# Twelve places instead of ten for the second stage's exponentials, in a gated cross-attention and self-attention kernel

## The reference

```python
x = x + tanh(g_xattn[0]) * xattn(layernorm(x), ctx_768, Wq, Wk, Wv, Wo, bo)
x = x + tanh(g_ffn[0]) * ffn(layernorm(x), Wq, bq, Wk, bk, Wv, bv, Wp, bp, ...)
# in ffn
q_norm = q / norm(q)
q_scaled = (q_norm + query_embedding) * softplus(temperature)
h = softmax(q_scaled @ k.T / sqrt(32)) @ v
gates = softmax(h @ Wr.T + br); top 3 of 15 routed heads, one shared head, two shared weights
out = (h * masked_gates.sum()) @ Wp.T + bp
```

## Time and profile before

| | us |
|---|---|
| median of 3 runs | 4596.27 (4593.71 to 4602.74) |
| the profiled execution | 4595.59 |
| its span, first to last instruction | 4593.8 |
| TensorE at work | 4350.3 (95%) |
| GpSimd | 3338.4 (73%) |
| VectorE | 2881.1 (63%) |
| ScalarE | 2528.2 (55%) |
| granted TensorE clock, mean | 0.985 |

### The profile page before, as it was taken

How to read it: one execution, slowest core, us unless ns; L and a number is a source line. 1 busy time by engine, 2 the same in 40 slices (tenths; PEclk the granted TensorE clock), 3 DMA queues, 4 the chain that set the end, 5 groups by cost and what they waited for, 6 DMA issues and landing times.

```text
span 4593.8 us, 67810 instructions
## 1 busy us (share of the span) xinstructions
PE 4350.3 (95%) x21568; PEld 2348.5 (51%) x21568; DVE 2881.1 (63%) x3955; ACT 2528.2 (55%) x4641; POOL 3338.4 (73%) x2667
## 2 busy tenths in 40 slices
PE   4899999999999999999999999999999999999997
PEld 3455555555555555554445444544454454544443
DVE  4455656464646464676777767676777667677661
ACT  2353535454535454546666666567557666565664
POOL 1566666767666667558888878778788879677897
PEclk7899999999999999999999999999999999999999
DMA  7476766666656666653435345354443454362532
GB/s 230 129 194 173 205 173 197 178 194 182 182 168 184 174 177 175 169 147 104 136 106 173 90 136 154 83 155 117 124 143 103 124 152 106 112 181 70 146 109 83
DMA packets 516175, 682.26 MB, mean 149 GB/s; under 512 B 42736, under 2 KB 371952, under 8 KB 506608
## 3 DMA queue, kind: packets, MB, share of 16 engines
q1 hardware_dynamic: 515824, 677.92, 52.7%
HBM read 323.57 MB, written 150.99 MB: 103 GB/s over the span
## 4 chain that ended last, share of the span: by engine, by line
PE 80%; issue 8%; ACT 4%; DVE 4%; POOL 2%; DMA 2%; SPq 0%; ACTq 0%; POOLq 0%; DVEq 0%
PE aux L957 28%; PE aux L1049 19%; PE aux L1063 18%; PE aux L1031 7%; PE aux L1075 4%; DVE nm L1404 2%; ACT probs L1247 2%; PE aux L1001 1%; POOL added_f L936 1%; PE aux L1083 1%; PE aux L977 1%; POOL added L936 1%; ACT more L1247 1%; DMA xs<-in_x 1%; DMA v_kept<-v_out 0%
## 5 line engine op out<-in xcount | busy, mean ns | idle before, releaser
L936 POOL TENSOR_TENSOR added<-added,probs 128x512 f32<-128x512 f32 x1433 | 1792.0, 1289 | 773.7 <-PE aux L1063 620.7
L1404 DVE TENSOR_REDUCE nm<-aux 128x2 f32<-128x1024 f32 x1536 | 1810.9, 1220 | 581.9 <-PE aux L1031 581.4
L1247 ACT ACTIVATE probs<-aux 128x512 f32<-128x512 f32 x2151 | 1172.3, 603 | 876.1 <-PE aux L1049 740.0
L1049 PE MATMUL aux<-stack 128*128 128x512 f32 x4096 | 1323.0, 427 | 76.5 <-ACT probs L1247 36.5
L1049 PEld LDWEIGHTS aux<-stack 128*128 128x128 f32 x4096 | 711.4, 189 | 740.7 <-issue 284.0
L1063 PE MATMUL aux<-probs,v 128*32 128x512 f32 (+1 forms) x4302 | 934.5, 610 | 4.3 <-ACT probs L1247 2.3
L936 POOL TENSOR_TENSOR added_f<-added_f,probs 128x512 f32<-128x512 f32 x537 | 672.3, 1287 | 119.6 <-PE aux L1063 73.8
L957 PE MATMUL aux<-xT_hi,wqk 128*128 128x512 f32 x1536 | 560.4, 404 | 1.0 <-ACT more L1247 0.6
L1031 PE MATMUL aux<-ck_hi,cq_hi 32*128 32x512 f32 (+1 forms) x3072 | 453.9, 483 | 53.3 <-DVE nm L1404 35.8
L1031 PEld LDWEIGHTS aux<-ck_hi,cq_hi 32*128 32x128 f32 (+1 forms) x3072 | 181.0, 185 | 512.4 <-issue 511.0
L957 PE MATMUL aux<-wvo,parts 128*128 128x512 f32 x1536 | 400.2, 403 | 10.6 <-issue 10.2
(11 more groups left out here) (132 smaller groups left out, 4387.4 us busy)
## 6 DMA issues: line engine op xcount, KB each, us to landing
wqk<-w_split SPq DMA_DIRECT2D x256, 256.0 KB, 3.8
wvo<-w_split SPq DMA_DIRECT2D x64, 1024.0 KB, 7.2
parts<-h_kept SPq DMA_DIRECT2D x128, 512.0 KB, 3.9
stack<-cq_hi SPq DMA_DIRECT2D x128, 256.0 KB, 5.2
stack<-ck_hi SPq DMA_DIRECT2D x128, 256.0 KB, 5.5
v_kept<-v_out SPq DMA_DIRECT2D x128, 256.0 KB, 2.3
v<-v_kept SPq DMA_DIRECT2D x64, 512.0 KB, 4.4
h_kept<-h_hi SPq DMA_DIRECT2D x128, 256.0 KB, 2.8
```

The lines of the kernel that those rows point to most:

```text
L936: pool.tensor_tensor(onto, onto, exp_buffer(T, e), ALU.add).then_inc(added_ok, 1)
L1049: ins = pe.matmul(out, stack[:, g % 2, e * ph.SLOTS + ks, jt * P:(jt + 1) * P], stack[:, g % 2, e * ph.SLOTS + qs, n * HALF:(n + 1) * HALF ...
L1247: act.activation(exp_buffer(T, e), aux[:, o.bank["S", T, e], :], ACT.Exp, scale=ph.SCALE).then_inc(probs_ok, 1)
L1404: dve.tensor_reduce(nm[:, half, first:first + 2 * TT - t:TT], aux[:, b:b + 2, :], axis=AX.X, op=ALU.max, negate=True).then_inc(emptied["dv ...
```

## The change

The second stage's ring has 12 places instead of 10 (`NP`), so `more` has five instead of three. The room comes from two tiles of 128 x 512 that are given up. `sq` goes: the squares and the squared reciprocal roots of a half lie in that half of `cq_lo` (function `squares`), which is written with the low parts afterwards. Therefore the Square (`pqa`) now waits until all copies of the group before into `stack` are in, and `ssa`'s wait takes over the one on the sums before. `bo_x` and `bo_f` become one tile `bo`: the second stage's bias is loaded (`bi`) and multiplied (`bm`) late in batch 8, after the last bias addition of the first stage. The product of ones waits, in the second stage, for the last exponential too. The planner's tables have other numbers in both stages; the number of instructions of each kind is the same on each engine.

```diff
-        self.NP = 10 if ffn else 7
+        self.NP = 12 if ffn else 7
...
-AT = (dict(p=[6.85, 18.67, 24.27, 59.8], over=16.35, held=1.78, mx0=-6.87, mxn=8.2, ctx=[5.28, 7.08, 92.2], load=[-42.24, -58.52], norm=[103.6, -14.1], turned=[33.14, 28.56], vp=[18.54, 5.67], out=[-1.35, 4.59], xr=35.76, split=-93.56,
...
+AT = (dict(p=[-7.28, -5.46, 26.71, 58.96], over=15.93, held=2.62, mx0=-6.98, mxn=11.77, ctx=[35.68, 9.54, 80.83], load=[-99.23, -37.63], norm=[65.32, -24.63], turned=[11.15, 41.85], vp=[13.57, 8.36], out=[0.46, 3.95], xr=110.22, split=-224.43,
...
+        self.add(("bi", 0), "sp", TURN * B + 50, [("xb", TT * B - 1)])
+        self.add(("bm", 0), "dve", TURN * B + 54, [("bi", 0)])
...
-            before = [("s3p", g - 1, n), ("pqa", g - 1, 1), earlier]
+            before = [("s3p", g - 1, n), ("pqa", g - 1, 1), ("sd", g - 1, last_head)]
...
-            self.add(("xb", t), "pool", b, [("xq", t) if half else ("xr", j), ("xb", t - 1)] + [("fb" if ph.ffn else "cd", 0)])
+            self.add(("xb", t), "pool", b, [("xq", t) if half else ("xr", j), ("xb", t - 1)] + [("bm" if ph.ffn else "cd", 0)])
...
-        qb, sq, qy, more, h_lo, bo_f, blk, wg, top, glog, gsum, added_f = earlier(
-            ("qb", [P, 2, HALF], F32), ("sq", [P, HALF], F32), ("qy", [P, HALF], F32), ("more", [P, F.NP - X.NP, HALF], F32), ("h_lo", [P, HALF], F32R),
-            ("bo_f", [P, DM], F32), ("blk", [P, P], F32), ("wg", [P, NG, GC], F32), ("top", [P, TT // 2, 8], F32),
+        qb, qy, more, h_lo, blk, wg, top, glog, gsum, added_f = earlier(
+            ("qb", [P, 2, HALF], F32), ("qy", [P, HALF], F32), ("more", [P, F.NP - X.NP, HALF], F32), ("h_lo", [P, HALF], F32R),
+            ("blk", [P, P], F32), ("wg", [P, NG, GC], F32), ("top", [P, TT // 2, 8], F32),
...
-        bo_x = sb("bo_x", [P, DM])
+        bo = sb("bo", [P, DM])
...
+        def squares(n):
+
+            return cq["lo"][:, n * HALF:(n + 1) * HALF].bitcast(F32)
...
+                    elif kind == "bi":
+
+                        sp.wait_ge(biased, TT * B)
+                        sp.dma_start(bo[:], small["bo_f"].partition_broadcast(P)).then_inc(b_in, 16)
...
+                        if ph.APART:
+                            pe.wait_ge(probs_ok, ph.scores(end - 1, G - 1))
...
-                        if (g, n) > (NG * B, 0):
-
-                            wait_emptied(act, ("ss", g, 0) if n else ("ss", g - 1, 1))
-                        act.activation(sq[:], src, ACT.Square, bias=bq[:, g % NG:g % NG + 1]).then_inc(sq_ok, 1)
+                        if n == 0:
+                            wait_stacked(act, g - 1, range(stage((g - 1) // NG).G))
+                        act.activation(squares(n), src, ACT.Square, bias=bq[:, g % NG:g % NG + 1]).then_inc(sq_ok, 1)
...
+                        if (g, n) > (NG * B, 0):
+
+                            wait_emptied(act, ("ss", g, 0) if n else ("ss", g - 1, 1))
...
-                        act.activation(sq[:], qy[:], ACT.Square).then_inc(y_ok, 1)
+                        act.activation(squares(n), qy[:], ACT.Square).then_inc(y_ok, 1)
...
-                        dve.wait_ge(f_in, 32)
+                        dve.wait_ge(f_in, 16)
                         link(dve.memset(blk[:], 0.0))
                         for e in range(F.G):
-                            dve.memset(blk[e * F.D:(e + 1) * F.D, e * F.D:(e + 1) * F.D], 1.0)
-                        dve.tensor_scalar(bo_f[:], bo_f[:], tg[:, 1:2], None, ALU.mult).then_inc(f_ok, 1)
+                            ins = dve.memset(blk[e * F.D:(e + 1) * F.D, e * F.D:(e + 1) * F.D], 1.0)
+                        ins.then_inc(f_ok, 1)
+                    elif kind == "bm":
+                        dve.wait_ge(b_in, 16)
+                        dve.tensor_scalar(bo[:], bo[:], tg[:, 1:2], None, ALU.mult).then_inc(b_ok, 1)
```

18 lines of the change are left out of this document (8 added, 10 removed), and 4 rows, old and new, of the table TAKES.

## The result

The changed kernel takes 4632.30 us (median of 3 runs, 4632.30 to 4636.20) against 4596.27 before: ratio 1.0083, 95% interval 1.0069 to 1.0097. I had forecast 4563. The profiled execution has a span of 4634.4 us, 40.6 longer; the mean granted clock fell from 0.985 to 0.980.

The account below looks back on a forecast made before the run. PE, at work 4350.3 of 4593.8 us, was taken as the bound, leaving its waits, lost clock and tile-shape changes to gain from. Terms -18 + 1 - 3 - 16 + 3 = -33 us gave 4563 us, range 4536 to 4594.

Parts of the forecast that it names:

- Term 1, the start: First batch of the first stage: first weighting 24 us earlier, remaining work +8, less low clock -2; sum -18 us.
- Rival (a): The start gives little because value weights land late and the values' load stays behind copies: -4, 4577 us; 17%.
- Term 2, the rest of the first stage: First stage after the start: order sums +4, less 3 for VectorE holding PE up less; +1 us, from -5 to +6.
- Term 3, the steady batches: Six middle batches of the second stage: -1 (sum), -3 (ring), +1.5 give -2.6 rounded each, -16 us in all.
- The ring: Second stage: two more places remove exponentials' waits for GpSimd's additions; 20 us taken, 3 per batch, bound 49.5.
- The order: Steady second-stage batches: PE's order sum gives -1 us per batch, tighter exponentials give back 1.5.
- Rival (c): Uneven halves the ring doesn't carry, and tighter exponentials, turn the steady batches' -16 into +15: 4594 us; 17%.
- First batch of the second stage: Second stage's first batch, 328.6 us before and as uneven after: -3 us.
- last batch: Second stage's last batch: four bias additions ahead of the last two halves +5, ring -2; +3 us.
- Edits with one answer: Squares in the low parts' place, new waits of the Square and denominators, moved bias load and multiply: 0 us.
- rival (d): The Square waits for its stack copies and holds up ACT, then PE; 62 us over 31 groups, 4625 us; 8%.
- Rival (b): Second stage's ring is worth its whole bound, 49.5 us instead of 20: 4534 us; 14%.

Follow-up runs that it names:

- plan12old: Changed kernel with the old planner tables in both stages and 12 ring places, order planned anew: 4596.51 us.
- froz12: Same as froz10, but the ring gets 12 places after the planning, the order still that of the kernel before: 4606.24 us.
- onep: Changed kernel with one second-stage table number, the first projection group's due time, put back from 4.32 to 3.46: 4622.41 us.
- froz10: Changed kernel's code with 10 ring places and the old order on PE, ACT and GpSimd; bias load and multiply placed by hand: 4608.37 us.

## Why the prediction was wrong

**Term 1, the start (-18; measured -12).** The first half of it held within 2 us: value weights waited for 0.55 us, first score 105.8 (107), first weighting 127.7 (126). A part of that is luck: the load of the values was issued 6.4 us after the eighth store, where I had counted 2.4. The term that was mis-sized is what remains of the batch after the first weighting, +8 - 2 in the working: 202.0 us before, 212.8 after, +10.8. The low part cost next to nothing beside VectorE: GpSimd took 2.34 to 2.36 us for each of the three at the start, the lower value of the earlier trace rows; the split that began 0.35 us before one of them ended took 2.50 us on VectorE instead of 2.29. Rival (a) did not occur.

**Term 2, the rest of the first stage (+1; measured +5.5).** At the edge of its range; the order sums had said +4, and the 3 us that I took off for VectorE didn't come. The runs say more than that: without the new first-stage table the second stage starts no later (2030.4 in plan12old), so the start's gain is a loan. I had looked at the two terms apart and not asked whether batches that end earlier run denser afterwards.

**Term 3, the steady batches (-16; measured +29.1).** This is the step that failed, in each of its parts. The ring, -3 per batch: following PE's waits back to a place gave 28 us, of which I took 20, and its bound of 49.5 had left out a fourth group of 5.7; froz12 removed 23 us of ACT's waits and the steady batches did not move. What stood behind a wait of PE was not what set it. The order, -1 + 1.5: wall went from 318.6 to 323.5. I had priced halves of the new pattern by like halves of the old order: 155 to 160 for the first four and 158.5 for the last four; they took 162.0 and 162.1. And the clock was not in the sum at all, though its column stood in every window. It had 2.9 us at the lower level per steady batch before and 12.5 after. By the two rates of the bounds above that is 1.8 to 4.8 us of the 4.9 that a batch lost, and by a third some 3; the rest is the order. What failed, then, is that waits were priced as if each were PE's, and that the clock was put at nothing. Rival (c), uneven halves with tighter exponentials, named the right place and the right sign, at +15; it lacked the clock, and onep shows that its own mechanism is small. The bound set in the prediction, "wrong if the steady batches exceed 319", is what was met.

**First batch of the second stage (-3; +4.8) and last batch (+3; +14).** In the first, PE is idle for 5.4 us behind the bias multiply; that is more than the 4.8 lost, and 8 were missed. The runs go from 324.7 to 350.5, and the four longest (342.8 and more) are the four in which the multiply took 11.8 to 13.7 us. The rest of the spread is the plan, and no rule of mine would have told it.

The last batch, counted to its last sums as in the prediction, went from 282.3 to 296.4, +14 instead of +3, and the finish behind them is 1 us shorter. GpSimd's last run of additions almost without a gap shows where this comes from. It began 132.1 us into the batch before and 136.9 in after; it then holds four bias additions more, 154.6 us instead of 150.1; and the sums, which came 0.1 us behind it, now come 4.9 behind, since twelve output matmuls more stand ahead of them on PE:

```profile
4589.36 5.37 PE L965 MATMUL aux<-wvo,parts 128*128 128x512 f32 x21
4596.14 3.00 PE L965 MATMUL aux<-wvo,parts 128*128 128x512 f32 x12 [1.41 <-issue]
4599.07 1.07 PE L1085 MATMUL aux<-added_f,ones 128*32 128x512 f32 x8
```

So the +5 for the bias additions was right (4.5); the -2 for the ring didn't come, and the late begin and the place of the sums were not in the term. Up to the last weighting it follows the second-stage table (273.1 and 273.7 us with the old one and 12 places, 285.6 and 285.7 with the new); the clock, 27.3 us at the lower level against 13.7, is in it too.

**Edits with one answer (0).** Right for the squares: squares in the low parts' place cost nothing (froz10), and rival (d) did not occur, since the Square waits for PE alone. The bias load and multiply are the other way: the 0 that I gave them, "far from use", was 5.4 us of idle PE in after and up to 12.8 in other runs, since on VectorE's queue the row maxima and the gates stand behind the multiply. Rival (b), the ring worth its whole bound, is excluded by froz12 for the order of before.

## What to carry to other kernels

Where PE is 95% busy, read the clock column by stretch and put it into the sum as a term: an order with a thin stretch ahead of a dense one pays twice. Don't price a ring or a buffer by the waits that end on it; hold the order fast and change it alone, and it may be worth nothing (2 us here), while the orders planned around the same 12 places ran from 4575 to 4649 us. An operation that is "far from use" still stands in its engine's order: look at what is behind it and at what the other engines do at that time. And when a change comes with new tables of numbers, take them stage by stage: here one table of the two, with the ring, gives 4575 us, and both give 4632.

## What the chip showed that I had not expected

Work added to PE can make a stretch shorter. Issuing 96 score matmuls twice (20 us of work over six batches) made the half behind each 16 of them 52.7 us long instead of 54.0 to 55.9, and the six batches of the profiled executions 10.2 us shorter, as the time at the lower clock fell from 75.1 to 34.1 us; the medians of the whole kernel are the same. 64 of them per batch cost 4 us in this order and 52 to 55 in one that was at full clock already. The drops come within a kernel whose PE is at work 95% of the span: after 4 us in which it issued 3 matmuls, the granted clock was 0.58 in the next 4.

A VectorE operation of half a microsecond, a multiply of 128x512 in float32 by one number per row, stood for up to 13.7 us while GpSimd added tile after tile, and ended 0.3 us after the last addition of the run in each of the eight traces in which it was long.
